# A three-layer graph network on one core: how TensorE waits for gathered rows, and how its work is cut, in layers two and three

## The reference

```
edge_in = x[src] * edge_weight[:, None]
agg = segment_sum(relu(edge_in @ W_msg + b_msg), dst)
x = layernorm(x + relu(agg @ W_out + b_out))            # layer one
e = x
for (w, SW, b) in ((w1, sl1, b1), (w2, sl2, b2)):       # layers two and three
    xt = einsum('nd,rde->rne', e, w)
    e = relu(segment_sum(xt[edge_type, src], dst) + e @ SW + b)
out = layernorm(x + e)
```

## Time and profile before

| | |
|---|---|
| median of 3 runs | 7084.83 us (7081.79 to 7088.7) |
| span of the profiled execution, first to last instruction | 6065.7 us |
| the profiled execution's own time with what lies around the span | not recorded; median less span is 1019.1 us |
| POOL busy | 4511.3 us, 74% |
| TensorE busy | 2683.3 us, 44% |
| DVE busy | 2607.2 us, 43% |
| ACT busy | 1031.7 us, 17% |
| gathers of layers two and three | 3152 |
| granted TensorE clock, mean of the span | 0.642 of full |

### The profile page before, as it was taken

How to read it: one execution, slowest core, us unless ns; L and a number is a source line. 1 busy time by engine, 2 the same in 40 slices (tenths; PEclk the granted TensorE clock), 3 DMA queues, 4 the chain that set the end, 5 groups by cost and what they waited for, 6 DMA issues and landing times.

```text
span 6065.7 us, 46678 instructions
## 1 busy us (share of the span) xinstructions
PE 2683.3 (44%) x11862; PEld 2109.9 (35%) x11862; DVE 2607.2 (43%) x4881; ACT 1031.7 (17%) x2878; POOL 4511.3 (74%) x4794
## 2 busy tenths in 40 slices
PE   6244555555555544444444444443333333333333
PEld 5233444444444332332323323233333333333333
DVE  6888888777555523333333333331222222222221
ACT  3333444444444300000000000000000000000000
POOL 7767777777777577777777777767777777777777
PEclk8666677766667666666666666665555555555555
DMA  6222323333233222222222222222222222222221
GB/s 182 61 86 80 99 89 100 92 91 91 86 92 89 81 70 80 81 77 81 77 81 80 77 81 77 81 79 57 59 60 60 59 60 59 60 59 59 60 59 57
DMA packets 279550, 471.55 MB, mean 78 GB/s; under 512 B 110125, under 2 KB 169385, under 8 KB 279270
## 3 DMA queue, kind: packets, MB, share of 16 engines
q0 software_dynamic: 152672, 312.98, 18.5%
q1 hardware_dynamic: 125446, 155.09, 7.4%
q10 hardware_dynamic: 1152, 0.39, 0.0%
HBM read 346.02 MB, written 122.09 MB: 77 GB/s over the span
## 4 chain that ended last, share of the span: by engine, by line
POOL 49%; issue 16%; PE 0%; DMA 0%; DVE 0%; POOLq 0%; ACT 0%; DVEq 0%; ACTq 0%; SPq 0%
POOL rows L749 49%; PE bank L1124 0%; POOLq L626 0%; DMA rows<-rel_table,rel_index 0%; PE bank L869 0%; DMA rel_table<-tab 0%; DVE picked L1175 0%; DMA rows<-msg_table,msg_index 0%; DVE tab L1215 0%; ACT tab L1056 0%; PE bank L1138 0%; ACT rows L697 0%; POOLq L136 0%; DVE stats L1242 0%; DVE y L1238 0%
## 5 line engine op out<-in xcount | busy, mean ns | idle before, releaser
L749 POOL DMA_INDIRECT rows<-rel_table,rel_index x3152 | 2973.8, 943 | 1010.7 <-issue 960.6
L749 POOL DMA_INDIRECT rows<-msg_table,msg_index x1555 | 1470.0, 945 | 508.5 <-issue 472.4
L869 PE MATMUL bank<-work,rows 128*128 128x128 f32 x6304 | 1149.7, 352 | 675.8 <-ACTq L720 675.8
L869 PEld LDWEIGHTS bank<-work,rows 128*128 128x128 f32 x6304 | 1079.6, 262 | 813.9 <-ACTq L720 752.0
L869 PE MATMUL bank<-onehot,rows 128*128 128x128 f32 x3238 | 673.8, 384 | 938.3 <-ACT rows L715 914.9
L1124 PE MATMUL bank<-wr,feat 128*128 128x512 f32 x784 | 627.1, 946 | 908.7 <-ACT feat L1082 892.2
L869 PEld LDWEIGHTS bank<-onehot,rows 128*128 128x128 f32 x3238 | 606.5, 283 | 1047.5 <-ACT rows L715 1011.3
L697 ACT ACTIVATE rows<-rows,weight 128x128 f32<-128x128 f32 x1555 | 494.8, 389 | 800.1 <-DVE onehot L816 484.4
L1124 PEld LDWEIGHTS bank<-wr,feat 128*128 128x128 f32 x784 | 216.7, 306 | 1113.5 <-ACT feat L1082 913.4
L1175 DVE TENSOR_TENSOR picked<-bank,chosen 128x512 f32<-128x512 f32 x392 | 265.3, 689 | 740.1 <-ACT tab L1056 733.3
L816 DVE TENSOR_TENSOR work<-bank,place 128x1024 f32<-128x1024 f32 x394 | 476.7, 1211 | 7.4 <-ACT agg L1034 3.7
(11 more groups left out here) (145 smaller groups left out, 1798.8 us busy)
## 6 DMA issues: line engine op xcount, KB each, us to landing
rel_table<-tab SPq DMA_DIRECT2D x196, 512.0 KB, 3.0
rows<-rel_table,rel_index POOLq DMA_INDIRECT x3152, 2.5
rows<-msg_table,msg_index POOLq DMA_INDIRECT x1555, 2.5
x_dram<-normed SPq DMA_DIRECT2D x98, 64.0 KB, 3.0
xin<-x_dram SPq DMA_DIRECT2D x98, 64.0 KB, 1.9
xin<-in_x_dram SPq DMA_DIRECT2D x97, 64.0 KB
out_dram<-normed SPq DMA_DIRECT2D x97, 64.0 KB, 1.6
tab<-in_x_dram SPq DMA_DIRECT2D x24, 256.0 KB, 4.6
```

Source lines behind the costliest of these rows:

```text
L749: nc.gpsimd.indirect_dma_start(rows[:, u, t, :], None, table, bass.IndirectOffsetOnAxis(ap=table_index[:, g, t:t + 1], axis=0)).then_inc(e ...
L869: ins = nc.tensor.matmul(total, tile, hot[:, t, :], start=t == 0, stop=t == most - 1)
```

## The change

In layers two and three of the sorted case:

- ACT no longer waits for rows and no longer counts `ready` (the calls of `act_ready` go).
- TensorE waits for the one-hot matrices and for each half group's rows itself (`pe_half_group`).
- TensorE's work is cut into pieces: two tiles, or 256 columns of a table product instead of 512. After each piece TensorE waits until that piece's result is written (`pe_piece`, or a wait on the semaphore that the piece counts up anyway), and only then goes on.
- In layer two, the first half of a block's table product stands between the two half groups of the group at whose step the block falls, and the second half behind that group (`pe_product`). For the last block, which falls behind the last group, both stand where they stood.
- Waits behind `pe_own` in the two layers' programs and behind the products of own rows.

The counter of the pieces is a semaphore that this path did not use (`s_dealt`). POOL's, DVE's and SP's instructions, their order and their waits are the same as before.

```diff
--- before.py
+++ after.py
@@ -279,6 +279,7 @@
         s_quad = sem("s_quad")
         s_dealt = sem("s_dealt")
         s_start = sem("s_start")
+        s_piece = s_dealt
 
         class NodeSems:
             def __init__(self, name, ln=False, table=False):
@@ -869,6 +870,29 @@
                     ins = nc.tensor.matmul(total, tile,
                                            hot[:, t, :], start=t == 0, stop=t == most - 1)
             ins.then_inc(sems.prod, 1)
+
+        pieces = [0]
+
+        def pe_piece(ins):
+
+            ins.then_inc(s_piece, 1)
+            pieces[0] += 1
+            nc.tensor.wait_ge(s_piece, pieces[0])
+
+        def pe_half_group(layer, sems, st, h):
+
+            hot, total = hot_of(layer, st), sum_of(layer, st)
+            if h == 0:
+                nc.tensor.wait_ge(sems.hot, st.n + 1)
+            nc.tensor.wait_ge(sems.rows[st.u][h], gathered(st, h))
+            for t in range(h * HALF, (h + 1) * HALF):
+                ins = nc.tensor.matmul(total, rows[:, st.u, t, :], hot[:, t, :], start=t == 0,
+                                       stop=t == TPG - 1)
+                if t % 2 and t < TPG - 1:
+                    pe_piece(ins)
+            if h:
+                ins.then_inc(sems.prod, 1)
+                nc.tensor.wait_ge(sems.prod, st.n + 1)
 
         def edge_step(eng, layer, sems, at, groups, lead, first):
             steps = groups // PAIR
@@ -1098,6 +1122,22 @@
             own = feat[:, 0:st.u + 1, :].rearrange("p u n -> p (u n)")
             nc.tensor.matmul(ps_self[:, 0:(st.u + 1) * P], ws[layer][:, :], own, start=True,
                              stop=not trim).then_inc(sems.own, st.u + 1)
+            if trim and layer:
+                nc.tensor.wait_ge(sems.own, st.n + 1)
+
+        def pe_product(layer, sems, st, h):
+
+            if h == 0:
+                nc.tensor.wait_ge(sems.feat, st.n + 1)
+            for k in range(2):
+                part = slice(k * H // 2, (k + 1) * H // 2)
+                ins = nc.tensor.matmul(ps_tab[h][:, part], feat[:, st.u, :],
+                                       wr[layer][:, h * H + part.start:h * H + part.stop],
+                                       start=True, stop=True)
+                if k == 0:
+                    pe_piece(ins)
+            ins.then_inc(sems.prod, 1)
+            nc.tensor.wait_ge(sems.prod, st.n * 2 + h + 1)
 
         def pe_nodes(layer, stage, trim):
             sems = node_sems[layer]
@@ -1119,11 +1159,16 @@
                                     ).then_inc(sems.t, 1)
             st = stage(PRODUCTS[layer]) if layer < 2 else None
             if st is not None:
-                nc.tensor.wait_ge(sems.feat, st.n + 1)
-                for h in range(2):
-                    nc.tensor.matmul(ps_tab[h][:, :], feat[:, st.u, :],
-                                     wr[layer][:, h * H:(h + 1) * H], start=True, stop=True
-                                     ).then_inc(sems.prod, 1)
+                if trim and layer == 1:
+                    first = layer == 1 and half_of(1, st.b) < COUNT[1]
+                    for h in range(int(first), 2):
+                        pe_product(layer, sems, st, h)
+                else:
+                    nc.tensor.wait_ge(sems.feat, st.n + 1)
+                    for h in range(2):
+                        nc.tensor.matmul(ps_tab[h][:, :], feat[:, st.u, :],
+                                         wr[layer][:, h * H:(h + 1) * H], start=True, stop=True
+                                         ).then_inc(sems.prod, 1)
                 if batch_end(st) and not (trim and short_batch(st)):
                     pe_own(layer, sems, st, trim)
             st = stage(PRODUCTS[layer] + 2) if trim and layer < 2 else None
@@ -1139,6 +1184,8 @@
                                            own_row_of(b, r), ident[0:r, :],
                                            start=False, stop=u == st.u)
                 ins.then_inc(sems.joined, st.u + 1)
+                if layer:
+                    nc.tensor.wait_ge(sems.joined, st.n + 1)
 
         def pe_own_message(half):
 
@@ -1809,16 +1856,19 @@
                     pe_trim(step)
                 if layer == 0:
                     pe_own_message(g)
-                pe_group(layer, edge_main, st)
+                    pe_group(layer, edge_main, st)
+                else:
+                    pe_half_group(layer, edge_main, st, 0)
+                    if layer == 1 and half_stage(1, g)(0) is not None:
+                        pe_product(1, node_sems[1], half_stage(1, g)(0), 0)
+                    pe_half_group(layer, edge_main, st, 1)
             elif eng is nc.scalar:
                 if layer == 0 and g == 0:
                     act_convert(0)
                 if layer == 0 and g + 1 < EARLY:
                     act_convert(g + 1)
-                if layer == 0 or g == 0:
+                if layer == 0:
                     act_ready(layer, edge_main, st)
-                if layer and group(g + 1) is not None:
-                    act_ready(layer, edge_main, group(g + 1))
 
         def fused_loop(eng, layer):
```

## The result

| | before | changed |
|---|---|---|
| median of 4 runs each | 7085.19 us (7081.79 to 7088.7) | 7343.93 us (7335.97 to 7358.77) |
| time of the profiled execution | not recorded | 7340.96 us |
| its span | 6065.7 us | 7339.2 us |

The changed kernel takes 1.0376 of the time before (95% interval 1.0363 to 1.0389): 259 us slower. The forecast was 7083.9 us, in a range of 7017 to 7106.

The account below looks back on a forecast made before the run. POOL's gather pace was taken to bound layers two and three; -1.4 us at layer two's end and +0.5 at layer three's gave -0.9 on a 6065.7 us span, plus 1019.1 carried over: 7083.9 us, range 7017 to 7106.

Parts of the forecast that it names:

- The carry-over of 1019.1 us: The runs' median of 7084.83 us exceeds the profiled span of 6065.7 by 1019.1; this was added unchanged, giving 7083.9.
- the middle of both layers: Layers two and three away from their ends: costs nothing, as TensorE's 15.8 of 19.98 us in layer two stays behind POOL.
- the restart of 0.40 us: TensorE's cost per extra piece: 0.14 us to see a result plus 0.26 for the load; seven more restarts, 2.8 us.
- POOL's pace: Layers two and three: a gather starts every 1.25 us (943 ns work, 0.30 issue) whatever other engines do; chance 0.62.
- The upper bound: Highest restart cost, 1.03 us, read from one product's end to the next through DVE and ACT.
- the second rival: TensorE becomes layer two's bound from a 1.0 us restart; at 1.2 us each +140 us, 7224; chance 0.06.
- The first rival: The 1019 us are spread over the gathers: a tenth back gives 7017 (chance 0.22), a tenth more 7152 (0.08).
- ACT lets go of the rows: Middle of a layer: `feat`, table-half copy and layer norm steps come up to 10 us earlier, worth nothing.
- The increments: Semaphore increments at about 26.3 ns each: seven more would be 0.18 us for two groups, hidden as well.
- The end of layer two: POOL's wait for layer three's table: POOL resumes at 4085.15 or 4086.95, 2.3 or 0.5 us sooner; 1.4 sooner taken.
- the forecast's other case: End of layer two: product 97 at the half clock takes 4.98 us, not 3.18, making the whole sum 0.0.
- the end of layer three: Last half group and block 96's transpose: one more restart and a wait, 0.40 + 0.14, 0.5 us later (0.3 to 1.2).

Follow-up runs that it names:

- r7: The changed kernel without TensorE's waits for its own results and their count-ups, on a late chip: 7034.42 us beside 7031.40 for the kernel before, ratio 1.0007.
- r4: The changed kernel without TensorE's waits for its own results and their count-ups, on a prompt chip: 6070.23 us beside 6075.08 for the kernel before, ratio 0.9993.
- r2: The kernel before with only the row waits moved from ACT to TensorE, on a prompt chip: 6071.98 us beside 6075.08 for the kernel before, ratio 0.9996.
- r8: The changed kernel without TensorE's waits for its own results, their count-ups kept, on a prompt chip: 6059.54 us beside 6065.42 for the kernel before, ratio 0.9989.
- r5: The whole changed kernel, run again on a prompt chip: 6066.68 us beside 6066.29 for the kernel before, ratio 1.0002.
- r12: The changed kernel without TensorE's waits for its own results, their count-ups kept, on a late chip: 7097.68 us beside 7077.10 for the kernel before, ratio 1.0028.
- r10: The whole changed kernel, once more on a prompt chip: 6067.14 us beside 6065.42 for the kernel before, ratio 1.0004.
- r11: The kernel before plus 12 idle ACT count-ups per group of layers two and three, on a late chip: 7101.82 us beside 7077.10, ratio 1.0034.
- r9: The kernel before plus 12 idle ACT count-ups per group of layers two and three, on a prompt chip: 6065.95 us beside 6065.42, ratio 1.0001.
- r3: The kernel before plus only two-tile pieces with waits for their own end, layers two and three, prompt chip: 6075.82 us beside 6075.08, ratio 1.0001.

## Why the prediction was wrong

**The carry-over of 1019.1 us** is the step that failed, and with it the nothing put down for the middle of both layers. "I carry these 1019.1 us over as they are" took them for a cost around the span; the gap of each profiled execution is 1.8 us. The profile of before belongs to the 6065 us level and its timed runs to the 7085 us level. So every number that was read from it (a result seen after 0.14 us, TensorE always done before POOL needs it) was a number of a prompt chip, used for a late one. What the sum has at nothing there, because the restart of 0.40 us is hidden behind POOL, measured 239 us more of POOL's waits for TensorE than without own waits (r7), of 259 in all; its waits for the two tables grew by 26 us (127.1 against 100.9). The Trainium skill, Runtime: NRT & Kernel Launch, section "The ~15µs preamble/postamble breakdown", gives 6.2 us by which a profile's total is longer than the reported time, and some 9 to 15 us around a kernel. In the runs the span is 1.8 us shorter than the time; the page's size, though not its figure, fits, and by it 1019 us had to be work.

**POOL's pace** was right on prompt chips: 944 ns and 480.3 / 1576 = 0.30 us, the spans 6065.5 and 6065.7. On the late chip the pace holds too, and the forecast said that the argument falls if 1.25 us changes. It did not change, and the argument fell: POOL's own pace is a bound only while TensorE frees the ring of eight groups in time, and that failed.

**The restart** of 0.40 us was right: 2.47 or 2.48 us against 2.08 for a half group in two pieces. Its parts were not: a result of the own engine is seen 0.06 us (58 ns) after its modelled end, not 0.14, and the gap to the next load shown is 0.35. The upper bound was misread too: the 1.03 us ahead of product 97 lie behind two instructions of ACT (0.69 and 0.30 us), not DVE and ACT. On the late chip it is another quantity. The gap from the end of a piece to the start of the next, behind a group's first and third piece, where TensorE waits for itself alone:

```text
                     layer two            layer three
                     first     third      first     third
prompt, median us    0.058     0.058      0.058     0.058
prompt, longest      0.059     0.059      0.059     0.059
late, median         0.058     0.058      0.058     0.059
late, mean           1.16      1.09       2.27      1.59
late, share over 1   21%       30%        31%       35%
late, longest        10.7      10.0       12.0      10.0
```

(784 of the 788 places in each profile.) The means are all above the 1.0 us that **the second rival** named as the point from which TensorE becomes the bound of layer two, and its sign came: POOL waits for L889. It had the mechanism, restarts too dear to be hidden, at a chance of 0.06, though not that most cost 58 ns and a fifth to a third over 1 us; "0.40 is far from 1.0" was true of a prompt chip only. It priced +140 us for layer two, where the layers' table has +179 over r7, and nothing for layer three, which has +100 (some 20 of the two are the chip's).

**The first rival** was right that the 1019 us were slowness inside the execution. It was wrong on where (POOL's pace, which never moved) and mostly on the sign: cutting TensorE's bursts gave back nothing (r7, r4), and its slower side, 7152 "from the many waits", is what came, larger. It had 0.08.

**ACT lets go of the rows**: worth nothing on the prompt chip, as forecast (r2, 0.9996), and on a late one nothing together with the new order and the cut products (r7, 1.0007); it was not run alone there.

**The increments** (the Trainium skill, TensorE: Matmul & The Clock Gate, section "The cost: per-tile semaphore tail", 26.3 ns each) would be, by an estimate, 36 us for 1378 if on the path. On a prompt chip they cost nothing (r8, -5.9 us), on a late one 20.6 us. The trace agrees with neither the full price nor, everywhere, with none.

**The end of layer two**, in the timeline of r5 on the prompt chip:

```profile
4069.01 2.47 PE L889 MATMUL bank<-work,rows 128*128 128x128 f32 x8 [0.50 <-DMA rows<-rel_table,rel_index]
4071.53 2.50 PE L1134 MATMUL bank<-wr,feat 128*128 128x256 f32 x4
...
4074.09 2.08 PE L1183 MATMUL bank<-ident,place 128*128 128x128 f32 x8
...
4077.30 5.03 PE L1134 MATMUL bank<-wr,feat 128*128 128x256 f32 x8 [1.13 <-ACT feat L1106]
...
4086.62 0.94 POOL L750 DMA_INDIRECT rows<-rel_table,rel_index  x1 [19.81 <-DMA rel_table<-tab]
```

POOL goes on at 4086.62 instead of 4087.45, inside the forecast's 4085.15 to 4086.95, but by luck: the gathers of layer two had ended 1.8 us sooner in this execution, and POOL's wait is 19.81 us, not the forecast 16 to 19. From the start of the last half group to POOL there are 17.61 us, before 16.62, forecast 14.32 or 16.12. So the end is 1.0 us later and not sooner. The terms that failed are those at the full clock: the half group took 2.47 and not 1.56, the own rows 2.08 and not 1.78, and product 97 5.03, the forecast's other case (4.98), all at a granted clock of 0.50. The Trainium skill, TensorE: Matmul & The Clock Gate, section "What's actually happening", by whose rule the prediction had that case, agrees here. At **the end of layer three** the last half group takes 2.48 us (+0.40 as said), and block 96's transpose begins 2.53 us behind its start, before 1.86: 0.67 later, where 0.5 was forecast (below, the same columns). Both ends are a microsecond, and the spans are 6065.5 and 6065.7.

```profile
6055.73 2.48 PE L889 MATMUL bank<-work,rows 128*128 128x128 f32 x8 [3.04 <-DMA rows<-rel_table,rel_index]
...
6058.26 0.47 PE L1152 MATMUL bank<-ident,sums 128*128 128x128 f32 x1
```

### What is shown, and what stays open

Shown: the loss needs both the own waits (r7 without them +3 us, r12 with their count-ups alone +21) and a late chip (r5, r10 with them 0), and it reaches the time as POOL's wait for `prod`. Shown as well: on late chips instructions of TensorE and ACT that wait for nothing are held for multiples of 0.70 us, POOL's gathers are not (98% or more start within 1.4 us of the one ahead in their group), and three quarters of the semaphore records are missing. What fits these, by argument: TensorE with no waits of its own has its instructions at hand, and makes up for a hold by running through what has gathered (0.112 us for a product and its load); with an own wait the next piece can't be begun until a held result is seen, so each hold comes onto TensorE's own path, until POOL's ring of eight groups is full.

What holds the instructions stays open. That the recording of the profile does it is a candidate: the Trainium skill, NOTIFIC — the notification-queue block, section "7.1 Overflow: three behaviours, one of which stalls the engine", has a setting in which a full queue of records stalls the engine that writes them, and the 0.70 us steps could look so. By the same section that setting drops no record, so the missing ones do not fit it. Against it stand also r11 (5 ns for each further instruction) and section "10. Constraints, capacities, measured rates" of the same page of the Trainium skill, by which a record costs the engine no time. Every execution here was recorded, so none tells whether an unrecorded one has the late level. Other causes, such as the supply of instructions to the engines or other work on the chip, were not tested.

No version beat both kernels: r2, r4 and r8 are within 0.2% of before on a prompt chip, and r8's kernel is 0.28% slower on a late one.

## What to carry to other kernels

Lay the profiled execution's span beside the runs' times before any other view: a gap of 17% of the span is no launch cost, and no wait read from that profile may be called hidden in those runs. A wait of an engine for its own result takes away its running ahead; at 58 ns it is free beside a slower engine, and where results can come late it puts each late one on the path, so keep none that nothing needs. Time a change in more than one session and on more than one chip: this one is 1.0002 on one and 1.0376 on another.

## What the hardware showed that was not expected

- The kernel before has two levels by chip: 6065 to 6075 us on three, 7031 to 7085 on the others, each steady within 0.5% in its one session.
- On late chips free instructions of TensorE and ACT are held at times, and then start in steps of 0.70 us (89% of the late count-ups on ACT in r11). Of TensorE's matmuls in layers two and three 20% follow the one ahead by over 600 ns in r11, and 12% in r9 on a prompt chip, those that wait for rows included. A gather still starts every 1.25 us (median of every late profile).
- A wait of TensorE for its own last product is passed 58 ns after that product's modelled end, at 784 places of r5 (longest 59), and up to 12.0 us after it on a late chip.
- The whole change lowered the granted clock from 0.67 to 0.55 in layer two (0.5 is the lower level of 1.2 GHz), and raised TensorE's busy time there by 621 us for 10% more instructions. No part alone lowered it as far: the groups' pieces with their waits had 0.71 there (r3, +151 us busy), the rows' waits 0.65 (r2), the change without own waits 0.64 (r4, +192 us busy).
- Without own waits on a late chip, others see TensorE's counts tens of us after its records say that the products ended: POOL 46 us (median, where it waits in layer three of r7), DVE up to 76 us.
